# Last cross attention of a four-layer decoder: product with the values in two runs a turn, value projections copied out by ScalarE, all scores of a pair lowered in one row on VectorE

## The reference

```
def _L3_xattn_ref(x, context, Wq, Wkv, null_kv, Wout, ln_scale, ln_bias):
    HEADS, DH = (16, 64)
    q = _split_heads(jnp.einsum('bnd,df->bnf', x, Wq))
    kv = jnp.einsum('bmc,cf->bmf', context, Wkv)
    k, v = jnp.split(kv, 2, axis=-1)                 # then split in heads
    k = jnp.concatenate((nk, k), axis=-2)            # one learned null key and value
    v = jnp.concatenate((nv, v), axis=-2)
    sim = jnp.einsum('bhid,bhjd->bhij', q * DH ** (-0.5), k)
    attn = jax.nn.softmax(sim, axis=-1)
    out = jnp.einsum('bhij,bhjd->bhid', attn, v)
    out = jnp.einsum('bnf,fd->bnd', out.transpose(0, 2, 1, 3).reshape(b, -1, INNER), Wout)
    ... # layer norm, scale and shift
```

## Time and profile before

| | us |
|---|---|
| median of 3 runs (4700.77 to 4709.14) | 4704.74 |
| the profiled execution | 4709.98 |
| its span in the profile | 4708.2 |
| busy in the span: PE, DVE, ACT, POOL | 3951.0, 3181.5, 2376.9, 1560.0 |
| mean granted TensorE clock over the span | 0.90 |

### The profile page before, as it was taken

One profiled execution on the slowest core, in us unless ns is written; L12 is line 12 of the kernel. 1 busy time (PEld: TensorE's weight loads), 2 busy tenths in 40 slices (PEclk: granted clock), 3 DMA queues, 4 the chain that ended last, 5 costly groups with the idle time before them and its releaser, 6 DMA issues. The chain is left out here.

```text
span 4708.2 us, 74527 instructions
## 1 busy us (share of the span) xinstructions
PE 3951.0 (84%) x28269; PEld 2412.2 (51%) x28274; DVE 3181.5 (68%) x5291; ACT 2376.9 (50%) x4528; POOL 1560.0 (33%) x1285
## 2 busy tenths in 40 slices
PE   3399999899189974888877899999999999999654
PEld 2133333388133333666664566666666666666442
DVE  3399899734277746333333688888888888888757
ACT  2288888733088852333331455555555555555330
POOL 0200000000300001111100477766777766677510
PEclk7599999999589986877778899999999999999877
DMA  5222222100255300000000100000000000000000
GB/s 166 62 47 52 45 48 43 26 16 16 41 88 87 58 2 27 0 0 0 0 8 11 46 15 1 15 1 15 1 15 1 15 1 15 1 1 1 6 19 31
DMA packets 119700, 123.06 MB, mean 26 GB/s; under 512 B 21264, under 2 KB 97648, under 8 KB 118992
## 3 DMA queue, kind: packets, MB, share of 16 engines
q1 hardware_dynamic: 119240, 118.27, 11.7%
q10 hardware_dynamic: 144, 0.52, 0.0%
HBM read 103.02 MB, written 15.73 MB: 25 GB/s over the span
## 5 line engine op out<-in xcount | busy, mean ns | idle before, releaser
L835 DVE TENSOR_REDUCE att_peak.1<-psS 128x1 f32<-128x512 f32 (+1 forms) x1024 | 580.7, 633 | 94.1 <-PE psS L705 94.0
L2498 POOL TENSOR_TENSOR key_sums_0.1<-key_sums_0.1,prob_0.1 128x512 f32<-128x512 f32 x256 | 415.5, 1623 | 28.7 <-POOL key_sums_0.1 L2498 0.4
L804 ACT ACTIVATE att_probT.1<-psT 128x512 f32<-128x512 f32 (+1 forms) x682 | 368.6, 568 | 74.7 <-PE psT L734 33.4
L2498 POOL TENSOR_TENSOR key_sums_1.1<-key_sums_1.1,prob_1.1 128x512 f32<-128x512 f32 x256 | 396.0, 1547 | 28.4
L835 DVE TENSOR_REDUCE att_peak.2<-psS 128x1 f32<-128x512 f32 (+1 forms) x512 | 266.9, 569 | 139.2 <-PE psS L705 137.1
L2337 ACT COPY prob_0.1<-psS 128x1024 f32<-128x1024 f32 (+1 forms) x224 | 203.7, 954 | 305.9 <-PE psS L2237 305.9
L705 PE MATMUL psS<-key_stack.1,query_stack.1 64*128 64x512 bf16 (+1 forms) x1024 | 270.8, 385 | 94.6 <-DMA key_stack.1<-key_parts 47.1
L2337 ACT COPY prob_1.1<-psS 128x1024 f32<-128x1024 f32 (+1 forms) x224 | 203.8, 954 | 283.3 <-PE psS L2237 283.3
L751 PE MATMUL psM<-att_probT.1,quad_values.1 128*9 128x256 f32 (+1 forms) x3840 | 306.4, 391 | 19.5 <-issue 19.5
L2407 DVE TENSOR_TENSOR att_highest.1<-att_highest.1,prob_1.1 128x1024 f32<-128x1024 f32 (+1 forms) x160 | 287.2, 1795 | 10.6 <-ACT prob_1.1 L2337 3.2
L2407 DVE TENSOR_TENSOR att_highest.1<-att_highest.1,prob_0.1 128x1024 f32<-128x1024 f32 (+1 forms) x160 | 284.2, 1776 | 11.9 <-ACT prob_0.1 L2337 5.3
(11 more groups left out here) (683 smaller groups left out, 9015.6 us busy)
## 6 DMA issues: line engine op xcount, KB each, us to landing
key_stack.1<-key_parts SPq DMA_DIRECT2D x384, 58.0 KB
key_stack.2<-key_parts SPq DMA_DIRECT2D x96, 200.1 KB
ctx_rows.1<-in_ctx_dram SPq DMA_DIRECT2D x8, 1536.0 KB
key_parts<-split_parts.1 SPq DMA_DIRECT2D x8, 1200.8 KB, 5.7
ctx_keys_0.1<-in_ctx_dram SPq DMA_DIRECT2D x4, 768.0 KB
ctx_keys_1.1<-in_ctx_dram SPq DMA_DIRECT2D x4, 768.0 KB
query_stack.1<-query_parts SPq DMA_DIRECT2D x192, 16.0 KB
ctx_values_0.1<-in_ctx_dram SPq DMA_DIRECT2D x4, 768.0 KB
```

The lines of the kernel that those rows point to most:

```text
L804: last = self.k.nc.scalar.activation(probs[:, blks[0]:blks[-1] + 1, :].rearrange("p b q -> p (b q)"), bank[0:w, 0:len(blks) * S], ACT.Exp)
L835: self.k.nc.vector.tensor_reduce(self.peak[:, 2 * h + s, c:c + 1], self.score_bank[m % 3][:, 0:w], AX_X, ALU.max).then_inc(self.peak_done. ...
L2498: nc.gpsimd.tensor_tensor(acc, acc, own[:, h, c * BANK:(c + 1) * BANK], ALU.add).then_inc(self.summed.sem, 1)
```

## The change

Three things change. MEETS becomes four chunks in the first group and three in the third, so the product stands in two runs instead of four. The copies of the value projections out of bank 0 go from VectorE to ScalarE, at the same places of the turn. And in VectorE's list the four lowerings of the second head follow those of the first at once; raise 1, which stood between them, comes behind, before raises 2 and 3.

```diff
--- before.py
+++ after.py
@@ -2085,7 +2085,7 @@
     CHUNKS = (KB + 1) // 2
     NULL = KTAIL + 1
     KEYS = KB * P
-    MEETS = [range(0, 2), range(2, 4), range(4, 6), range(6, 7)]
+    MEETS = [range(0, 4), (), range(4, 7), ()]
 
     def __init__(self, k, mem):
         self.k = k
@@ -2312,9 +2312,14 @@
 
 
     def act_take(self, act, name):
-        k, nc, bank = self.k, self.k.nc, self.bank[1]
+        k, nc, bank = self.k, self.k.nc, self.bank[self.number[name][0]]
         kind, of, n = name
         self.wait_made(act, name)
+        if kind == "value":
+            if n < 3:
+                last = nc.scalar.copy(self.val[of % 2][:, 4 * n:4 * n + 4, :].rearrange("p t c -> p (t c)"), bank)
+            else:
+                last = nc.scalar.copy(self.val[of % 2][0:KTAIL, KB - 1, :], bank[0:KTAIL, 0:P])
         if kind == "key":
             w = BANK if n < 3 else KTAIL
             last = nc.scalar.copy(self.keyT[of % 2][:, n * BANK:n * BANK + w], bank[:, 0:w])
@@ -2324,7 +2329,7 @@
             c, g = n // 4, n % 4
             w = BANK if g < 3 else KTAIL
             last = nc.scalar.copy(self.ctxT[of % 2][:, c, g * BANK:g * BANK + w], bank[:, 0:w])
-        last.then_inc(self.taken[1].sem, 1)
+        last.then_inc(self.taken[self.number[name][0]].sem, 1)
 
     def act_keep(self, act, i, s):
         k, nc = self.k, self.k.nc
@@ -2344,7 +2349,7 @@
 
     def act_take_at(self, act, i, at):
         for x, name in enumerate(self.due(i, at)):
-            if name is not None and (at + x) % 2 == 1:
+            if name is not None and (name[0] == "value" or (at + x) % 2 == 1):
                 self.act_take(act, name)
 
     def act_run(self, act):
@@ -2375,11 +2380,6 @@
         k, nc, bank = self.k, self.k.nc, self.bank[0]
         kind, of, n = name
         self.wait_made(dve, name)
-        if kind == "value":
-            if n < 3:
-                last = nc.vector.tensor_copy(self.val[of % 2][:, 4 * n:4 * n + 4, :].rearrange("p t c -> p (t c)"), bank)
-            else:
-                last = nc.vector.tensor_copy(self.val[of % 2][0:KTAIL, KB - 1, :], bank[0:KTAIL, 0:P])
         if kind == "ctx":
             c, g = n // 4, n % 4
             w = BANK if g < 3 else KTAIL
@@ -2390,7 +2390,7 @@
 
     def dve_take_at(self, dve, i, at):
         for x, name in enumerate(self.due(i, at)):
-            if name is not None and (at + x) % 2 == 0:
+            if name is not None and name[0] != "value" and (at + x) % 2 == 0:
                 self.dve_take(dve, name)
 
     def dve_raise(self, dve, i, s):
@@ -2454,16 +2454,12 @@
             if softmax:
                 for part in range(4):
                     self.dve_lower(dve, i - 1, 0, part)
+            if softmax:
+                for part in range(4):
+                    self.dve_lower(dve, i - 1, 1, part)
+            self.dve_take_at(dve, i, 2)
             if scores:
                 self.dve_raise(dve, i, 1)
-            if softmax:
-                self.dve_lower(dve, i - 1, 1, 0)
-                self.dve_lower(dve, i - 1, 1, 1)
-            self.dve_take_at(dve, i, 2)
-            if softmax:
-                self.dve_lower(dve, i - 1, 1, 2)
-                self.dve_lower(dve, i - 1, 1, 3)
-            if scores:
                 self.dve_raise(dve, i, 2)
                 self.dve_raise(dve, i, 3)
             self.dve_take_at(dve, i, 3)
```

## The result

The changed kernel takes 4723.94 us (median of 6 runs, 4710.84 to 4726.98), the kernel before 4705.36 us on the same chips: a ratio of 1.0035, with a 95% interval of 1.0024 to 1.0045. It is slower, by 16.5 us by the ratio (18.6 by the two medians), where the text above forecast 4697 us. The profiled execution took 4726.98 us, its span is 4725.2.

The account below looks back on a forecast made before the run. The prediction took TensorE's own order to bound the kernel, busy 1730 of 1753 us. Its terms, -40.3 - 5.6 + 38.6 = -7.3 us, gave about 4697 us, with a range of 4676 to 4712 us.

Parts of the forecast that it names:

- Fewer runs of the product: TensorE's product in two runs saves gaps between array forms: 0.65 us a turn over 62 turns, -40.3 us.
- The wait for the peak: TensorE's wait at L2251 for VectorE's peak goes in plain turns: 33 x 0.17 us, -5.6 us.
- VectorE's row: VectorE loses value copies, raise 1 slows to 2.15 us beside GpSimd; context copy 0.2 us later, at 16.8 us.
- signs of being wrong: Raise 1 of 1.2 us, plain turn over 27 us, wait at the sum of keys, or L2217 waiting for ScalarE's copy.
- raise 1 stays at 1.22 us: Faster rival, chance 0.22: GpSimd waits instead of VectorE's raise 1, context copy 0.9 us sooner, 4678 us.
- The slow rival: Chance 0.12: each VectorE raise pays a whole GpSimd addition, 2.5 us; sum +31 us, 4735 us.
- The context turns: Third value projection waits 1.84 us longer for VectorE's context copy in 21 turns: +38.6 us.
- ScalarE's copies: Value copies moved to ScalarE cost nothing as long as TensorE does not wait for the bank.
- The two ends: Ends of the stage shift by up to one product run: nothing taken, 2 us either way in the range.

Follow-up runs that it names:

- four_runs_b: Changed kernel with the context copy between raises 1 and 2 and the product back in four runs: 4703.5 us, 0.9996 of the kernel before.
- both_early: Changed kernel with the context copy between raises 1 and 2 and the division directly behind the reciprocal: 4655.4 us, 0.9902 of the kernel before.
- best: both_early with ScalarE emptying the transposed context's bank before the value projection's at place 2: 4648.7 us, 0.9883 of the kernel before.
- divide_early: Changed kernel with VectorE's division moved directly behind the reciprocal, ahead of raises 4 and 5: 4710.2 us, 1.0019 of the kernel before.

## Why the prediction was wrong

From the first mark to the last the change cost 17.3 us, where the sum had -7.3. Step by step:

- **Fewer runs of the product, -40.3 us.** Right: 0.64 us a turn, four_runs_b against both_early, in plain turns without their wait and in those with an output projection; in turns with context, against best, 0.5 to 0.7 us.
- **The wait for the peak, -5.6 us.** The wait at L2251 went, as said. But this is the step that failed: "Margin 1.2 us; what would be late next is this same peak." What was late next was the division. The first chunk of the product waits for it, and the product now starts 1.72 us earlier against VectorE's row. By the prediction's own turn of 26.6 us and run of 32 the product would be ready at 26.6 - 3.6 = 23.0 us after the mark. The division would end at 16.8 + 1.67 + 3.73 + 0.41 = 22.6, with the reciprocal at 16.8 as predicted and the rest from the kernel before (from the reciprocal to raise 4, 3051.70 - 3050.03; raises 4 and 5 from start to start, 3055.43 - 3051.70; the division): a margin of 0.4 us, which the prediction never worked out. Then raises 4 and 5 took 4.23 us, start to start, instead of 3.73, since raise 4 met an addition of GpSimd nearer to its beginning, and the division ended at 23.2. It costs 0.32 us a plain turn, 33 x 0.32 = 10.6 us; divide_early confirms it. None of the prediction's signs of being wrong would have shown this wait.
- **VectorE's row.** The forecast put the context copy at 16.8 us after the mark, 16.95 was measured; raise 1 at 2.15, 2.21 measured. The rival "raise 1 stays at 1.22 us" is out. The slow rival, every raise at 2.5 us, is out too (2.10 us in the median, 2.29 at most), but its idea, that the exclusion costs more than the mean says, came true in raises 4 and 5.
- **The context turns, +38.6 us.** The mechanism was right and the largest term. The wait grew by 28.8 us (42.6 - 13.8), 1.37 us a turn and not 1.84, so that it is 1.8 to 2.3 us long and not the 2.4 to 2.9 given as a sign. The 0.55 us for ScalarE's context copy, 21 times, came ahead of it and shortened it, as the prediction had said. Together they are 40 us. With the transitions such a turn is 1.36 us longer instead of 1.19, so 3.6 us over the 21.
- **ScalarE's copies, nothing.** Right: no value projection waits for ScalarE's copy in the turns counted.
- **The clock, not in the sum.** Three slow stretches cost 31.24 - 29.67 = 1.57, 32.14 - 30.52 = 1.62 and 32.03 - 30.52 = 1.51 us: 4.7 us.
- **The two ends, nothing, 2 us either way.** The first turn became 2.15 us longer (25.29 for 23.14), 1.2 us of it from the start of its last product run on, which has 32 matmuls and not 16; where the rest comes from is open. The last one with scores was put among the plain ones, 0.65 us shorter; it became 2.9 us longer (28.87 for 25.97), since the division held the product 4.26 us (2.57 before) and the run of 32 then went at the lower clock. Together 2.15 + 3.55 = 5.7 us.

10.6 + 3.6 + 4.7 + 5.7 make up the 24.6 us between -7.3 and +17.3. The wait for the division is the largest of them, and most of the last turn's part comes from it too. The measured 4723.9 us lies above the range's end of 4712 us, since neither the wait for the division nor the clock was in any of its cases.

## What to carry to other kernels

When work on the engine that sets the time is moved forward, list every wait of the moved instructions, and work out for each one when its condition is met; a margin for the wait that is going away says nothing on the others. A copy that frees a bank belongs directly behind the moment its data is ready, ahead of long work whose result is wanted later: here two calls moved in VectorE's list turned a loss of 17 us into a gain of 46. Where an operation and one of another engine exclude each other, its price is no mean: work it out for the place, from what the other engine has in course there.
